# Gather stage of a graph layer: places in the blocks unpacked once, picks read through a register's column

## What is computed

```python
norm = dinv[row_sl] * ew_sl * dinv[col_sl]
xw = h6_all @ W
msgs = xw[col_sl] * norm[:, None]
h7 = jax.ops.segment_sum(msgs, row_sl, num_segments=N) + b
```

```python
qkv = (x @ w_qkv + b_qkv).reshape(B, HW, HEADS, 3 * HEADC)
kv = jnp.einsum('bhnd,bhne->bhde', k, v) / HW
```

## Time and profile before

| | us |
|---|---|
| median of 3 runs | 4517.35 (4515.73 to 4520.52) |
| the profiled execution | 4502.67 |
| its span, first to last instruction | 4500.9 |
| the gather stage in it, first to last gather issue | 1020.6 to 3509.3 |

### The profile page before, as it was taken

The page is one execution under the profiler, slowest core; times in us unless marked ns, Lnnn a source line. Parts: engine busy times, 40 slices in busy tenths (PEclk is TensorE's granted clock), DMA queues, the critical chain, the costliest instruction groups (busy, mean ns, idle before and its releaser), DMA issues. The chain is left out here.

```text
span 4500.9 us, 75623 instructions
## 1 busy us (share of the span) xinstructions
PE 3399.5 (76%) x20283; PEld 2597.3 (58%) x20283; DVE 2931.0 (65%) x7496; ACT 1429.0 (32%) x4439; POOL 2770.0 (62%) x2543
## 2 busy tenths in 40 slices
PE   7677777246777777777756777777777589999995
PEld 6455554243444444444435666566665479999885
DVE  8899998674565565655655555555555665555676
ACT  2455554440111111111002222222322255555442
POOL 0488888436666666666666666666666245555553
PEclk9678787557888888888868888888888799999998
DMA  2111111763333333333334444444446612222466
GB/s 76 17 3 3 3 3 3 239 228 116 110 108 111 110 112 108 111 110 111 109 89 119 128 131 131 130 130 132 128 130 121 139 46 70 68 70 68 148 217 215
DMA packets 285822, 472.50 MB, mean 105 GB/s; under 512 B 95011, under 2 KB 180778, under 8 KB 285743
## 3 DMA queue, kind: packets, MB, share of 16 engines
q0 software_dynamic: 140544, 273.69, 24.5%
q1 hardware_dynamic: 138047, 193.90, 12.7%
q10 hardware_dynamic: 7154, 3.99, 0.3%
HBM read 350.11 MB, written 123.70 MB: 105 GB/s over the span
## 5 line engine op out<-in xcount | busy, mean ns | idle before, releaser
L1621 POOL DMA_INDIRECT rows<-table,idx x1664 | 1675.1, 1007 | 815.5 <-issue 497.3
L1904 DVE TENSOR_TENSOR acc<-acc,ps_seg 128x256 f32 x1664 | 695.5, 418 | 955.5 <-remote 761.6
L2069 PE MATMUL ps_seg<-rows,pick 128*128 128x256 f32 x3328 | 997.3, 429 | 272.0 <-DVE acc L1904 182.0
L2069 PEld LDWEIGHTS ps_seg<-rows,pick 128*128 128x128 f32 x3328 | 660.4, 213 | 514.0 <-issue 404.6
L771 POOL DMA_INDIRECT records<-sort_rec,sort_addr x280 | 528.8, 1889 | 260.7 <-DVE sort_rec L874 158.7
L1746 DVE TENSOR_SCALAR pick<-iota_row,loc,ewt 128x128 f32<-128x128 f32 x1680 | 529.2, 363 | 5.6 <-remote 1.8
L2509 POOL DMA_INDIRECT y_rows<-arena,idx x212 | 249.8, 1178 | 290.0 <-DVE arena L2556 185.2
L2641 PE MATMUL ps_h<-arena,up_now 128*128 128x128 f32 x3392 | 417.8, 277 | 0.0
L2625 PE MATMUL ps_y<-down_now,arena 128*128 128x256 f32 x1696 | 401.4, 380 | 0.0
L2641 PEld LDWEIGHTS ps_h<-arena,up_now 128*128 128x128 f32 x3392 | 398.3, 193 | 1.9
L926 PE MATMUL ps_out<-acc 128*128 128x240 bf16 x1568 | 281.5, 364 | 142.0 <-DVE acc L860 141.9
(11 more groups left out here) (385 smaller groups left out, 5122.7 us busy)
## 6 DMA issues: line engine op xcount, KB each, us to landing
rows<-table,idx POOLq DMA_INDIRECT x1664
acc<-y_rows SPq DMA_DIRECT2D x28, 640.0 KB
xn<-xn_dram SPq DMA_DIRECT2D x100, 128.0 KB
table<-acc SPq DMA_DIRECT2D x98, 128.0 KB
xT_dram<-xT SPq DMA_DIRECT2D x98, 128.0 KB
xn<-xT_dram SPq DMA_DIRECT2D x49, 256.0 KB
skip<-skip_dram SPq DMA_DIRECT2D x49, 256.0 KB
x_rows<-acc SPq DMA_DIRECT2D x49, 256.0 KB
```

Source lines behind the costliest of these rows:

```text
L1621: pool.indirect_dma_start(out=rows[:, t, :], out_offset=None, in_=k.table, in_offset=bass.IndirectOffsetOnAxis(idx[:, h, t:t + 1], 0), bou ...
L1904: dve.tensor_tensor(here, here, sums(u), ALU.add).then_inc(added[u], 1)
L2069: last = pe.matmul(sums(t), pick[:, h, t, :], rows[:, t, :], start=True, stop=True)
```

## The change

- The place in the block, `loc`, is unpacked once for all 1680 columns (`locate`): first for the 16 of step 0, and after step 0's picks are made, for the other 1664. It is a shift to int32 in the buffer of `loc`, and a conversion in the same buffer. `unpack` keeps only the index.
- The weight is no longer copied: `ew` is a view of word 1 of the records. `ewt`, `loc_i` and `ewt_done` are gone.
- `make_pick` takes both scalars at the column `n * 16 + t`. In a loop that column is in a register.
- `k.places` was one row of 1664 words; it is now two rows (partitions 0 and 32) of 832 words, even steps in one and odd steps in the other. The load from DRAM is two DMAs of 52 pieces of 64 bytes.
- `t1`, `t2`, `t3` and `kvT` lie in the four slots of `xT`, and `from_sums` waits until these slots have been stored.

```diff
-            k.places = k.sb("places", [1, TILES], I32, kv_consts)
+            k.places = k.sb("places", [P // 4 + 1, TILES // 2], I32, kv_consts)
...
-                sp.dma_start(k.places[:, :], k.places_dram.rearrange("(o b) t -> o (b t)", o=1)).then_inc(places_in, 16)
-                sp.wait_ge(places_in, 16)
+                for h in range(2):
+                    sp.dma_start(k.places[h * (P // 4):h * (P // 4) + 1, :].rearrange("o (b t) -> o b t", t=STEP_TILES),
+                                 k.places_dram.rearrange("(b h) t -> h b t", h=2)[h:h + 1, :, :]).then_inc(places_in, 16)
+                sp.wait_ge(places_in, 32)
...
-        loc_i = sb("loc_i", [P, 2, STEP_TILES], I32)
-        loc = sb("loc", [P, 2, STEP_TILES])
-        ewt = sb("ewt", [P, 2, STEP_TILES])
+        loc = sb("loc", [P, TILES + STEP_TILES])
+        ew = k.recs[:, :, 1].bitcast(F32)
...
-        t1 = sb("t1", [P, DC, P])
-        t2 = sb("t2", [P, DC, P])
-        t3 = sb("t3", [P, DC, P])
...
-        kvT = sb("kvT", [P, DC, P])
+        t1, t2, t3, kvT = (xT[:, q, :, :] for q in range(LOOKAHEAD))
...
-                    now = k.recs[:, bass.ds(n * STEP_TILES, STEP_TILES), :]
-                    dve.tensor_scalar(idx[:, h, :], now[:, :, 0], (1 << DST_BITS) - 1, None,
-                                      ALU.bitwise_and).then_inc(idx_done, 1)
-                    dve.tensor_scalar(loc_i[:, h, :], now[:, :, 0], DST_BITS, None,
+                    now = k.recs[:, bass.ds(n * STEP_TILES, STEP_TILES), 0]
+                    dve.tensor_scalar(idx[:, h, :], now, (1 << DST_BITS) - 1, None, ALU.bitwise_and).then_inc(idx_done, 1)
+
+                def locate(part, done):
+                    dve.tensor_scalar(loc[:, part].bitcast(I32), k.recs[:, part, 0], DST_BITS, None,
                                       ALU.logical_shift_right).then_inc(loci_done, 1)
-                    dve.tensor_copy(ewt[:, h, :].bitcast(I32), now[:, :, 1]).then_inc(ewt_done, 1)
-                    dve.wait_ge(loci_done, n + 1)
-                    dve.tensor_copy(loc[:, h, :], loc_i[:, h, :]).then_inc(loc_done, 1)
-
-                def make_pick(h, t):
-
-                    made = dve.tensor_scalar(pick[:, h, t, :], k.iota_row[:, :], loc[:, h, t:t + 1], ewt[:, h, t:t + 1],
+                    dve.wait_ge(loci_done, done)
+                    dve.tensor_copy(loc[:, part], loc[:, part].bitcast(I32)).then_inc(loc_done, 1)
+
+                def make_pick(h, n, t):
+
+                    at = bass.ds(n * STEP_TILES + t, 1)
+                    made = dve.tensor_scalar(pick[:, h, t, :], k.iota_row[:, :], loc[:, at], ew[:, at],
                                              ALU.is_equal, ALU.mult)
...
-                        k.places[0:1, bass.ds(n * STEP_TILES, STEP_TILES)], engines=[dve.engine], min_val=0,
+                        k.places[h * (P // 4):h * (P // 4) + 1, bass.ds(n * SLOT - h * SLOT, STEP_TILES)], engines=[dve.engine], min_val=0,
...
                     dve.wait_ge(k_all_summed, 1)
+                    for q in range(LOOKAHEAD):
+                        dve.wait_ge(xT_out[q], 16 * (FULL + (LEFT + q < BLOCKS)))
...
                 unpack(0, 0)
+                locate(slice(0, STEP_TILES), 1)
                 dve.wait_ge(loc_done, 1)
                 for t in range(STEP_TILES):
-                    make_pick(0, t)
+                    make_pick(0, 0, t)
+                locate(slice(STEP_TILES, TILES + STEP_TILES), 2)
+                dve.wait_ge(loc_done, 2)
...
-                    places = places_of(n)
+                    places = places_of(n, h)
 
                     start_after(dve, summed_up[SLOT - 1], n)
                     unpack(1 - h, n + 1)
-                    dve.wait_ge(loc_done, n + 2)
                     for t in range(STEP_TILES):
-                        make_pick(1 - h, t)
+                        make_pick(1 - h, n + 1, t)
```

More of the change, by code:

```diff
@@ L1495, in gather_and_mix @@
         added = [k.sem(f"tile_added{t}") for t in range(STEP_TILES)]
-        (idx_done, loci_done, loc_done, ewt_done, gather_held) = (
-            k.sem(name) for name in "idx_done loci_done loc_done ewt_done gather_held".split())
+        (idx_done, loci_done, loc_done, gather_held) = (
+            k.sem(name) for name in "idx_done loci_done loc_done gather_held".split())
         (kv_consts, k_turned, k_xT, k_kv, k_raw, k_sq, k_ss, k_sd, k_rs, k_rsv, k_scaled, k_summed, k_all_summed) = (
```

2 lines of the change are left out of this document (1 added, 1 removed).

## The result

The changed kernel takes 4536.38 us (median of 6 runs, 4532.53 to 4537.80), the kernel before on the same chip 4514.81 us (6 runs, 4512.70 to 4520.52). The ratio is 1.0045 with a 95% interval of 1.0034 to 1.0056: slower by some 20 us. The profiled run of after took 4537.80 us, with a span of 4536.1.

What follows compares the result with a forecast made beforehand. POOL's gathers were taken to bound the kernel, 20.9 us a step plus 319 us of stalls. Profiled 4502.67 - 4.6 + 0.6 = 4498.7; on the median 4517.35 - 4.0 = 4513 us, no change, range 4482 to 4540.

Steps and rivals of the forecast that it cites:

- the cost of the register instructions: DVE's picks in the gather stage: 31 a step at 57 ns, covered by adds and picks, so costed at nothing.
- the register instructions set DVE's pace: Rival, DVE in the gather stage: uncovered register instructions make the kernel slower, 4533 to 4548 us; chance 0.12.
- Its point of decision: Register rival's test on DVE: it holds if a pair of tiles in a bunch takes more than 1.40 us.
- a slope of 0.21: Gather stage: at most 0.21 us of step time per us of DVE work, from windows without side work and kv.
- The saving: DVE's step boundary: three instructions and a wait go, 0.42 us a step, 43.7 us at most; 4.6 us taken.
- The places: End of setup: a second transfer issue and 104 pieces instead of one row cost 0.6 us, between 0.2 and 1.5.
- The large unpacking: DVE after step 0's picks: shift 1.18 us, conversion up to twice that; step 0 starts 3.5 to 4.6 later, hidden.
- The signs that I had named: Profile after: gathers 1.305 us, POOL's waits 300 to 320, last gather 3505 to 3510, DVE busy down up to 58.
- The rule that the prediction weighed: POOL shares SBUF interfaces with DVE, so fewer DVE instructions could give it up to 58 us; prediction took nothing.
- Fetches: Rival, DVE's longer loops: bodies fetched anew each iteration, 106 us at most, up to 4619 us; chance 0.03.
- the remote waits: Gather stage: 291.5 us of POOL's stalls; the prediction would be wrong if they hang closely on DVE's timing.

Runs made afterwards that it cites:

- fixed_columns: The changed kernel with the picks' place and weight copied once a step into small buffers and read at fixed columns; 4485.78 us, ratio 1.0006 to before.
- registers_alone: The changed kernel with the three small unpacking instructions and their wait put back in every step, results unused; 4509.53 us, ratio 1.0055 to before.
- after_again: The changed kernel unaltered, run once more in a job where before took 4205.97 us; 4206.67 us, ratio 1.0007.
- semaphores_instead: The kernel before with two unread semaphore increments ahead of every pick on DVE, no register instructions added; 4548.02 us against 4519.69, ratio 1.0070.
- paced_before: The kernel before with four unread semaphore increments ahead of every gather on POOL; 4583.99 us, ratio 1.0094 to before.

## Why the prediction was wrong

**The sum.** Forecast were 4513 us and no change, inside a range of 4482 to 4540. It came out at 4536, slower, inside the range and by way of a rival with a chance of 0.12.

**The step that failed** is the cost of the register instructions, "I cost them at nothing". Its price was 57 ns each, taken from the last stage, which has indirect transfers but no crowded stretch, and its cover was reckoned from quick bunches. Outside of crowded stretches both hold well enough: the two instructions of a pick take 99 and 40 ns at the median, 0.14 us in place of 0.11, and a pair keeps its 1.40 us. Inside them each takes 0.72 us. Then a pair has four more of them, 2.9 us, and no cover of 0.3 us hides that; and instructions that were quick in before are slow beside them (199 of the 393 slow records). In place of nothing they cost what separates after from `fixed_columns`, 1.0045 less 1.0006: 0.39% or 18 us, across two jobs. In one job `registers_alone` less `fixed_columns` gives 0.49%.

**The rival that came out** ("the register instructions set DVE's pace", 4533 to 4548) was right in size. Its point of decision, a pair of over 1.40 us in a bunch, was right too, but it holds in some 100 stretches and not everywhere, and its arithmetic (1.4 us in every step by a slope of 0.21) hit the size by luck. What the traces show: 282 us of slow instructions came in, DVE's remote waits fell by 278 us, and some 20 us came through. So most of the slow instructions fell into time in which DVE had waited for TensorE anyway. They show as PE's waits for DVE's adds, 182.0 us and now 240.2, and as POOL's stalls.

**The saving** of 0.42 us a step was real where it could be seen: 0.33 us between index and first pick without gathers, and 0.17 us from index to pick in after, as forecast. Taken were 4.6 us. `registers_alone` less after is 0.1%, 4.5 us, which agrees but is no more than the uncertainty of each, and the two were timed in different jobs.

**The places** were taken at 0.6 us, bounded by 1.5. They cost 1.6. The end of `setup` in after, beside the earlier trace rows:

```profile
138.90 1.67 SPq L375 DMA_DIRECT2D places<-places_dram  x2
143.06 0.06 DVE L818 MEMSET sort_own<- 128x1 f32 x1 [6.18 <-PEq L122]
```

Issuing 52 pieces took 0.7 to 0.9 us, while a whole row had taken 0.21. The one row was the wrong one to count by. The first gather starts later by more than this, 2.4 us; the rest I can't tell from spread, for in `after_again`, with the same transfers, it starts at 1020.6 as in before. **The large unpacking** was hidden as forecast. The shift took 1.16 us (estimated 1.18) and the conversion 1.03, less than the estimate of 1.2 to 2.4:

```profile
1026.63 1.16 DVE L1737 TENSOR_SCALAR loc<-recs 128x1664 int32<-128x1664 int32 x1
1027.83 1.03 DVE L1740 CAST loc<-loc 128x1664 f32<-128x1664 int32 x1
...
1044.24 0.97 DVE L1907 TENSOR_TENSOR acc<-acc,ps_seg 128x256 f32 x2 [2.71 <-issue]
```

By 1044 us DVE stands idle again. Together these one-time costs are the 0.06% of `fixed_columns` and the 0.07% of `after_again`; both intervals reach to no change.

**The signs that I had named.** The gathers kept 1.305 us. POOL's waits came to 351 us (324.8, 19.9 for the index and 6.1 for TensorE by name) where 300 to 320 were forecast, and the last gather to 3534.3 where 3505 to 3510 were. DVE's busy time did not fall by 58 us but stayed (2931.0, now 2930.5). A pick of after takes 369 ns at the mean in place of 363, which makes 11 us; the crowding can't be the whole reason, since without gathers the busy time fell by 2.2 us only (2889.1 to 2886.9), and I can't account for the rest. The rule that the prediction weighed, POOL gaining where DVE does less, is not borne out: gathers have a median of 998 ns in after and 1002 in before. Fetches played no part: between 1110 and 2180 us one instruction packet moved, in place of none.

**The deeper fault** is one that the prediction named itself: the remote waits "whose cause I can't see". Where the crowding is absent, the stalls are absent too: `fewer_waits`, which is before less one wait in each pair, goes from first to last gather in 2178.1 us with the crowding away, against 2488.7. DVE's own trace hardly showed the crowding in before (3 slow records), but SyncE's did, with 95, and the trace was at hand: a look at the longest instructions of every sequencer in the stage, and not only of the one that the change loads, would have shown a price of 0.7 us beside that of 57 ns. I counted four more small instructions at their undisturbed price in a stage that 319 us of unexplained stalls had shown to be disturbed.

**What stays open.** The gathers must be there for the crowding, but what it is that they fill is not shown, nor why `experts` with its indirect transfers is free of it, nor why it was absent in two of the jobs, nor why DVE's own instructions are slow only where it has more of them than in before. That the direct form would not crowd is untested, as both runs of it fell into uncrowded jobs; so is whether four more instructions a pair cost more on TensorE. Nothing explains either why TensorE with more instructions was 0.14% faster, twice. No kernel here beats before where the engines are crowded.

One candidate, not shown here: the price falls on instructions of DVE, POOL and SyncE, is much the same for a register and a semaphore, and doesn't change with bytes. The Trainium skill (NOTIFIC — the notification-queue block, section 7.1, Overflow: three behaviours, one of which stalls the engine) says that the block which writes the records of instructions holds its producers back inside rather than lose a record, and that this could throttle an engine. If so, the crowding would belong partly to the recording. Against it speak ScalarE, whose sequencer has no slow record, and `experts`, where more instructions come in a microsecond and none is slow. Every run here gives a span and a granted clock, so none can be set against one without records.

## What to carry to other kernels

An instruction that only writes a register or a semaphore was free here only while its engine's sequencer ran at its undisturbed pace, so take its price from the same stage and look at the maximum beside the median, on the sequencers of all engines. Where a stage has remote waits whose cause is unseen, count the small instructions that a change adds to each engine there, and prefer a copy of a few hundred nanoseconds once a step to a register instruction for every use, as `fixed_columns` did with neither loss nor gain. When two jobs disagree, look at the kernel before in both: here its time, 4520 or 4210 us, told whether the loss could show at all.

## What was not expected of the hardware

In crowded stretches small instructions of the sequencer took 0.72 us each on DVE (393 in after, 596 in `semaphores_instead`), as much on POOL (880 in `paced_before`, 0.71 us each) and on SyncE (95 in before, 0.75 us each), whether they write a register or raise a semaphore, and none of ScalarE's did. Without gathers, the register instructions ahead of picks took 40 to 111 ns. In `experts`, with an indirect transfer in every 2.1 us, none of DVE's took over 92 ns. With the slow instructions that a kernel adds, others that were quick without them turn slow (308 of the 596). A quarter of the bytes per gather and at most four gathers in flight changed nothing in this. One unchanged kernel took 4520 us in one job and 4206 us in another on a chip of the same number, and its gather stage, by that of `fewer_waits`, was 310 us shorter. And a transfer into one partition in 52 pieces took 0.7 to 0.9 us to issue against 0.21 us for one piece.
